# Cross-attention block: a hand-written order for the first eight slots, and the V projection of batches 2 to 5 made there in plain fp32

## The reference

```python
q, k, v = proj(x, Wk, bk), proj(ctx, Wk, bk), proj(ctx, Wv, bv)     # one weight for q and k
scores  = q @ k.T / sqrt(32)
p       = softmax(where(allow, scores, NEG)) * allow
dist    = sqrt(clip((sum(p) - cumsum(p)) * |i - j|, 0))
effect  = clip(exp(dist * -softplus(gammas)), 1e-5, 1e5)
attn    = softmax(where(allow, scores * effect, NEG))
x1      = layer_norm(x + concat(attn @ v) @ Wo.T + bo, ln1)
out     = layer_norm(x1 + relu(x1 @ W1.T + b1) @ W2.T + b2, ln2)
```

## Time and profile before

| | |
|---|---|
| three executions | 1573.33, 1573.59, 1576.73 us (median 1573.59) |
| the profiled execution | 1576.78 us, span of its trace 1575.0 us |
| busy, share of the span | PE 94%, PE weight loads 78%, DVE 74%, ACT 66%, POOL 7% |
| mean granted clock of PE | 0.972 of full |
| the first 187.2 us (startup and slots 0 to 7) | PE busy 120.4 us, DVE 138.1 us, ACT 116.4 us |
| DMA | 334 MB, 212 GB/s in the mean |

### The profile page before, as it was taken

How to read it: one execution, slowest core, us unless ns; L and a number is a source line. 1 busy time by engine, 2 the same in 40 slices (tenths; PEclk the granted TensorE clock), 3 DMA queues, 4 the chain that set the end, 5 groups by cost and what they waited for, 6 DMA issues and landing times.

```text
span 1575.0 us, 34730 instructions
## 1 busy us (share of the span) xinstructions
PE 1476.0 (94%) x13056; PEld 1232.7 (78%) x13056; DVE 1165.7 (74%) x3971; ACT 1037.4 (66%) x2679; POOL 102.6 (7%) x97
## 2 busy tenths in 40 slices
PE   4567899999999999999999999999999999999897
PEld 3455788878878887887888788788878878888786
DVE  5787769687787968778696877869687786968533
ACT  2776766766667676666767666676766667676622
POOL 4000101000010100001010000101000010100000
PEclk8777999999999999999999999999999999999999
DMA  5774556555665655565555556656555665654776
GB/s 214 245 250 186 191 186 213 206 197 201 213 221 197 220 202 194 203 213 219 198 221 204 191 203 218 220 191 226 201 189 207 216 222 190 223 201 176 269 290 255
DMA packets 62790, 334.13 MB, mean 212 GB/s; under 512 B 8224, under 2 KB 8224, under 8 KB 29472
## 3 DMA queue, kind: packets, MB, share of 16 engines
q1 hardware_dynamic: 62624, 331.92, 58.6%
HBM read 306.72 MB, written 25.17 MB: 211 GB/s over the span
## 4 chain that ended last, share of the span: by engine, by line
PE 64%; DVE 26%; ACT 7%; issue 1%; DMA 1%; POOL 1%; SPq 0%; POOLq 0%; DVEq 0%; ACTq 0%
PE bank L205 18%; PE bank L207 16%; PE bank L206 16%; PE bank L401 7%; DVE w_sb L1028 6%; DVE w_sb L1016 5%; PE bank L415 4%; DVE gz L1024 2%; DVE w_sb L1038 2%; DVE s_sb L1004 1%; ACT w_sb L698 1%; ACT w_sb L700 1%; PE bank L437 1%; ACT w_sb L696 1%; DVE rows L1098 1%
## 5 line engine op out<-in xcount | busy, mean ns | idle before, releaser
L205 PE MATMUL bank<-xt_hi,w_ring 128*128 128x256 f32 x1024 | 296.0, 289 | 0.9 <-ACT h_sb L777 0.9
L207 PE MATMUL bank<-xt_hi,w_ring 128*128 128x256 f32 x1024 | 287.7, 281 | 0.0
L206 PE MATMUL bank<-xt_lo,w_ring 128*128 128x256 f32 x1024 | 287.2, 281 | 0.0
L719 ACT COPY pt_sb<-bank 128x512 f32<-128x512 f32 x192 | 111.8, 582 | 203.7 <-PE bank L415 203.6
L1004 DVE CUSTOM_DVE_ANT_0 s_sb<-bank,mask 128x256 f32<-128x256 f32 (+7 forms) x512 | 129.9, 303 | 155.4 <-PE bank L401 154.4
L205 PE MATMUL bank<-w_ring,h_hi 128*128 128x512 f32 x512 | 211.3, 413 | 7.9 <-DVE h_lo L1111 6.4
L689 ACT ACTIVATE w_sb<-s_sb,nm 128x161 f32<-128x161 f32 (+7 forms) x512 | 164.1, 404 | 77.7 <-DVE nm L1012 77.7
L709 ACT ACTIVATE p_sb<-w_sb,nm 128x32 f32<-128x32 f32 (+7 forms) x512 | 205.7, 405 | 0.0
L207 PE MATMUL bank<-w_ring,h_lo 128*128 128x512 f32 x512 | 203.9, 398 | 0.0
L206 PE MATMUL bank<-w_ring,h_hi 128*128 128x512 f32 x512 | 202.5, 396 | 0.0
L401 PE MATMUL bank<-qk_sb 32*32 32x256 f32 (+7 forms) x4096 | 170.5, 294 | 33.6 <-DVE m L1004 27.1
(11 more groups left out here) (130 smaller groups left out, 2989.5 us busy)
## 6 DMA issues: line engine op xcount, KB each, us to landing
w_ring<-w_split SPq DMA_DIRECT2D x256, 1024.0 KB, 4.8
w_split<-w_ring SPq DMA_DIRECT2D x32, 512.0 KB, 5.1
x_raw<-x_t SPq DMA_DIRECT2D x16, 512.0 KB, 3.9
c_raw<-ctx_t SPq DMA_DIRECT2D x16, 512.0 KB, 5.0
u_sb<-x_rows SPq DMA_DIRECT2D x16, 512.0 KB, 5.9
ring_raw<-w SPq DMA_DIRECT2D x32, 256.0 KB, 5.6
out<-rows SPq DMA_DIRECT2D x15, 512.0 KB, 6.9
wk_raw<-wk SPq DMA_DIRECT2D x1, 1024.0 KB, 4.8
```

The source lines that it names most:

```text
L205: nc.tensor.matmul(dst, a_hi, b_hi, start=start, stop=False)
L206: nc.tensor.matmul(dst, a_hi, b_lo, start=False, stop=False)
L207: return nc.tensor.matmul(dst, a_lo, b_hi, start=False, stop=stop)
L719: nc.scalar.copy(pt_sb[:, n], pt_bank[:]).then_inc(pt_ok, 1)
```

## The change

- **A list of its own for slots 0 to 7.** Each engine has a function `first`, which takes the place of the calls of `step` for batches 0 and 1. `over_batches` calls `first()` and then `step` from batch 2 on.
- **V ahead.** In slots 2 to 6 PE makes V of batches 2 to 5 (`values_ahead`, eight halves) in plain fp32, 4 matmuls of 512 columns each, from unsplit copies of Wv (`ahead_w`) and of the context (`ahead_c`), which SP loads. ACT copies the results, SP stores them to DRAM and loads them again in slot 3 of the step before. `step` leaves out `values` and `value_rows` for these batches.
- **Splitting the feed-forward weights.** The rounding moves from ACT to POOL. The tiles come in the order 4 to 15, then 0 to 3, of which the last four stay in `w_ring`, so the first loads of pairs 0 and 1 go. `SPLIT_BY` sets how many are done in each slot: 0, 3, 3, 2, 2, 4, 2, 0. The load of the tile at place `at + 3` is issued after the store of the one at place `at`.
- **Startup.** Wk is loaded, rounded and split in two parts (128 columns, then 384), the inputs are loaded between them, the gammas come by ACT's queue, and POOL's constants are made in another order, waited for in four steps.
- **In `step`.** On DVE in slot 3 `mask_scores(i, 3, 0)` and `(i, 3, 1)` come ahead of `rows_low(i - 1, 0)` and `concat_low(i, 0)`. In the last step `hidden_low(B - 2, 1)` comes right behind the running sums.
- **In `final`.** The second half of the last projection goes to the transposes' bank, which saves a wait for the first half's residual. `turn_rows` comes ahead of `add_hidden(ffn, 6)`, and `hidden(last, 0)` ahead of `add_hidden(ffn, 7)`.

The diff, cut: the ranges of batches and tiles; `values_ahead` and slot 2 of PE's `first`; PE's `step`; POOL's `split_high`; slots 5 and 6 of DVE's `first`; PE's `final`.

```diff
-            for i in range(B):
-                step(i, True, 1 <= i, 2 <= i, 3 <= i, i + 1 < B)
+            first()
+            for i in range(2, B):
+                step(i, True, True, True, 3 <= i, i + 1 < B)
...
+        SPLIT = [*range(4, FT), *range(4)]
+        SPLIT_BY = (0, 3, 6, 8, 10, 14, 16, 16)
         def split_in(n):
-            return range(3 * n, 3 * n + 3) if n < 4 else range(2 * n + 4, 2 * n + 6) if n < 6 else ()
+            return range(SPLIT_BY[n - 1] if n else 0, SPLIT_BY[n])
...
+            def values_ahead(k, t):
+                if t == 0:
+                    if k == 0:
+                        pe.wait_ge(ahead_w_in, 16)
+                    pe.wait_ge(ahead_c_in[k % 2], 16 * (k // 2 + 1))
+                if k > 0:
+                    pe.wait_ge(ahead_ok, RT * k - 1 + t)
+                at = slice(P * t, P * t + P)
+                for m in range(KT):
+                    mm = nc.tensor.matmul((h_bank, y_bank[0])[t][:], ahead_c[k % 2][:, m, at], ahead_w[:, m],
+                                          start=m == 0, stop=m == KT - 1)
+                mm.then_inc(ahead_mm, 1)
...
+            def first():
...
+                scores(0, 2, 0)
+                scores(0, 2, 1)
+                pe.wait_ge(const_ok, CONSTS)
+                transposes(0, 0, 0)
+                scores(0, 2, 2)
+                pe.wait_ge(qk_ok, 3)
+                queries_keys(0, 3)
+                transposes(0, 0, 1)
+                values_ahead(0, 0)
+                transposes(0, 0, 2)
+                attend(0, 0)
+                values_ahead(0, 1)
...
-                if ahead:
+                if ahead and i + 1 not in AHEAD:
                     pe.wait_ge(qk_ok, NQ * i + 5)
                     values(i + 1, 0)
...
+            def split_high(at):
+                n = SPLIT[at] % 4
+                pool.wait_ge(raw_in[n], 32 * (at // 4 + 1))
+                nc.gpsimd.tensor_copy(w_ring[:, n::4, 0], ring_raw[:, n::4, 1]).then_inc(ffw_hi_ok, 1)
...
+            def first():
...
+                totals(1, 0)
+                masks(1, 2)
+                splits(5)
+                residual(0, 0)
+                residual(0, 1, y_bank[1])
+                moments1(0)
+                weigh1(0)
+                shift1(0)
+                decayed_scores(1, 1)
+                rows_low(0, 0)
+                rows_low(0, 1)
+                running_sums(1, 2)
+                splits(6)
...
+                hidden(last, 0)
                 add_hidden(ffn, 7)
-                hidden(last, 0)
```

More of the change, by code:

```diff
@@ L202, in build, with made @@
         TURN_BANKS = ((h_bank, pj_bank), (pj_bank, h_bank))
+        def made(i):
+            return RT * sum(b not in AHEAD for b in range(i))
         def three_passes(dst, a_hi, a_lo, b_hi, b_lo, start, stop):
@@ L823, in step @@
                     deviation2(i - 3)
-                if now:
+                if now and i not in AHEAD:
                     value_rows(i, 1)
@@ L1250, in final @@
                 totals(last, 2)
-                hidden_low(ffn, 1)
                 moments2(B - 3)
```

540 lines of the change are left out of this document (419 added, 121 removed).

## The result

The changed kernel takes **1557.20 us** (median of 4, 1555.57 to 1559.33) against 1573.65 (1573.33 to 1576.73) for the kernel before in the same comparison: ratio 0.9885, 95% interval 0.9873 to 0.9897. The forecast was 1535 with a range of 1515 to 1558. So the direction was right and the time lies just inside the range, but less than half of the forecast gain came. The profiled execution took 1558.47 us with a span of 1556.7, 18.3 less than the span before; the sum had said 39.0.

The account below looks back on a forecast made before the run. The prediction took waits and DVE to bound the first stage, then steps of PE's work followed by a DVE chain. Its terms, -12 - 9.5 - 5.5 - 11.2 + 6 - 6.8 = -39.0, gave 1535 us (median), range 1515 to 1558.

Parts of the forecast that it names:

- Term 1: Startup: running sums first at 20.5 us instead of 32.49; -12 us, bounds -8 to -14.
- Term 2: First to eighth running sums: 134 us instead of 143.5, bounded mainly by DVE's work; -9.5 us.
- 118.6 + 7 + 1.5 + 7 = 134: First to eighth running sums: DVE's work, POOL's roundings beside it, the ring's wait and PE's V, in us.
- the floor of 118.6: DVE's own work between first and eighth running sums: 115.6 us plus Wv's subtraction, 2.3, and one h_lo, 0.7.
- the ring's wait: DVE stands 4 to 6 us for place 13's load; 1.5 net, since the residual waits for two projections anyway.
- the last term, 7: First stage: 7 us for PE's eight plain fp32 halves of V, mostly hidden, and for waits on ACT's copies.
- Term 3: Eighth running sums to batch 2's first scores: 5.5 us instead of 11.1; -5.5 us.
- Terms 4 and 5: Batches 2 to 5: V saved in slot 0, -11.2 us; stops where slot 3's V is gone, +6 us.
- The charge of 2.0 per stop: Slot 3, batches 3 to 5: PE stands 4.0 us, low clock follows; 2.0 us per step, bounds 0 to 2.7.
- Term 6: The end: the 4.10 us stop shrinks by 2.6, the clock holds, waits of 0.85 and 0.93 go; -6.8 us.
- C: First stage: POOL's roundings count in full and the ring's wait stands open, +10 and +4; 1549 us, chance 0.17.
- B: Batches 2 to 5: clock holds in the stops and DVE's chain has air, V saved whole; 1521 us, chance 0.15.

Follow-up runs that it names:

- act_rounds: The change with the sixteen roundings of the W1 and W2 pairs moved back from POOL to ACT; 1556.25 us.
- adds_early: The change with POOL's two sums (b2 to LayerNorm's bias, bo to the first batch's rows) ahead of the roundings, as before the change; 1559.07 us.
- third_limit: The change with the eleventh subtraction a group earlier, V ahead's eighth half in front of scores(1, 2, 2), and its last store and copy earlier; 1552.99 us.
- third_act2: third_limit with the sixteen roundings on ACT and two groups of them earlier in ACT's list, V ahead whole; 1551.61 us.
- best_act2: The change with the edits of half_ahead, third_limit and end_load, the roundings on ACT and two groups of them earlier in its list; 1538.39 us.
- best_masks: best_act2 with slot 3's two masks back at the place of the kernel before; 1535.42 us, ratio 0.9742.
- third_act: third_limit with the sixteen roundings on ACT, V ahead whole; 1552.41 us.
- half_ahead: The change with only slot 0's half of V made ahead for batches 3 to 5, slot 3's half again in three passes; 1549.66 us.
- end_load: The change with SP loading the last batch's third pair of W1 before it waits for add_hidden(ffn, 7); 1554.21 us.
- masks_exact: The change with slot 3's two masks back between concat_low(i, 0) and rows_low(i - 1, 1), as in the kernel before; 1553.10 us.

## Why the prediction was wrong by half

*Term 1, startup, a size.* x landed for POOL's rounding at 7.83, c at 9.74, and PE began at 10.27, where 1.25 MB had been put at "some 6 us". Queries and keys were 2.8 us later than forecast, the running sums 2.6 later. No run tested it.

*Term 2, the step that failed: "118.6 + 7 + 1.5 + 7 = 134".* DVE's time in the stage adds up to the 145.6 us measured as follows: 131.9 busy, which is the floor of 118.6 and 13.3 of stretch; 6.2 of waiting for the ring; 7.5 of other idle time. So the stretch was 6.3 us more than its term, the ring's wait 4.7 more than its net, and the last term, 7, was right in size.

The stretch by POOL was put at 0.6 us for each of twelve roundings. The price held (act_rounds: 9.0 us for sixteen, 0.56 each), the count did not: all sixteen fall behind the first running sums, and the sum had no term for the rest of POOL's work, some 4 us. The price itself was read from the wrong pair of rows. In the earlier trace rows the cast of 0.77 us begins 0.70 us before the rounding of 1.04 us shown below it. Beside them in the trace of the kernel before stand:

```profile
79.92 2.69 POOL L1308 CAST x_hi<-x_raw 128x1024 fp32r<-128x1024 f32 x1 [51.81 <-DMA x_raw<-x_t]
82.67 0.94 DVE L1051 TENSOR_TENSOR zi_pair<-z,zi_pair 128x8 fp32r<-128x8 f32 x1
```

The DVE cast ended with the rounding that had begun at 79.92, and the next instruction of DVE, with two inputs, 0.17 us alone, ended with the rounding of 1.04 us: 0.77 us of stretch, not 0.6. That the mean came out near 0.6 is luck in part, since some roundings stretched nothing.

The form of the sum failed too: each wait was priced as if the others' cover stayed, and then the prices were added. What covered the ring's wait, "the residual behind it waits for two projections on PE anyway", was itself late, by 4.4 us of masks and a half of V at low clock, both counted elsewhere or as hidden. So this group ended with the latest of several chains: the ring, the projections, and V's last store, 7.15 us to land, on which ACT waits (the prediction had V's DMA as "beside loads" and did not ask where SP issues it). One edit at a time moved the eighth running sums earlier by 0 to 1.5 us, which is within their scatter (adds_early moved them later, by 2.9).

Of the 11.6 us missing in this term, the runs with the whole of V ahead gave 5.9 back: 3.2 with the limits of this group gone (third_limit) and 2.7 more with the roundings on ACT and called early (third_act2). Three halves of V less gave 3 to 5 more (best_act2, best_masks), and with that the stage takes 137.2 and 135.2 us, near the 134 of the forecast. So V's being hidden held for the change as it is, and not once its other waits go. How the 5.9 us split between stretch and waits stays open, since ACT's list puts waits in the stretch's place (act_rounds, third_act).

*Term 3* held, 0.9 us better than forecast.

*Terms 4 and 5.* The mechanism held in every part: stops of 4.0 to 4.4 us, 1.2 in batch 5, low clock behind, nothing from the masks. The charge of 2.0 per stop was too small, and so was its upper bound of 2.7 in this execution: 2.5 to 3.1 by the windows, 2.8 by half_ahead. That is 2.4 of the 3.0 us missing here. Over all profiles with such stops the loss was 1.4 to 3.2 us, so the bound was not far off. The steps that were to lie "near 89 to 91" are 91.2, 91.9 and 91.7 for batches 3 to 5.

*Term 6.* The stop fell by 2.4 of the 2.6 forecast. The other 4.2 were taken back by a wait that the prediction had not looked for: `hidden(last, 0)` was moved ahead of `add_hidden(ffn, 7)` on PE, but SP's list still waited for the latter before it loaded the pair for `hidden(last, 2)`. 1.86 us, and low clock for one group of 24 matmuls (0.66 on the mean from 1510 to 1515; 4.4 us from its start to the next group's instead of 2.9). end_load gives 3.5 of the 4.2 back.

*The rivals.* None came whole. C named the two things that were in the stage, the roundings "in full" and the open wait, but each alone was worth 0.8 to 1.5 us when it was taken away, not 14. B (V saved whole) happened once, in one step of masks_exact, where the clock happened to hold.

*The steps from batch 5 to batch 14* were to keep 91.7 us; they take 91.76 against 91.73.

## What to carry to other kernels

Where several chains meet in one group of work, do not add the prices of their waits: write down when each would end with the others gone, and take the latest; an edit that takes away one alone may measure as nothing, which does not prove that its wait does nothing. And when a price per piece comes from a trace, look which two pieces overlap in it, and count every piece that will fall into the stage. A piece of work that fills a stop of the busiest engine is free, and taking it away can cost as much as its own length through the clock. When an instruction is moved on one engine, follow every queue that waits for its signal, the DMA issuer's above all.
